# Cross-attention of layer 0 in a four-layer kernel: scores formed a second time with keys on partitions, so that the exponentials need no transpose

## The chip, the cores and the metric

The kernel is one program on one core of a Trainium2 chip. The metric is device microseconds (us) of one execution, the median of several. All numbers below come from one profiled execution of the kernel before the change, or from its three timed runs.

## The reference, cut to what matters

Four layers follow each other, each an attention from B=4 sequences of S=256 tokens (D=256) to a context of T=64 tokens. The change is in layer 0, whose keys are the 64 context tokens and the 256 tokens themselves (320 keys), with 16 heads of 16:

```python
h = jnp.concatenate([x, latents], axis=1)
q = (latents @ q_w + q_b).reshape(b, k_len, NH, DH)
kv = (h @ kv_w + kv_b).reshape(b, p + k_len, NH, DH, 2)
kmat, v = (kv[..., 0], kv[..., 1])
attn = jnp.einsum('bkhd,bnhd->bhkn', q, kmat) / DH
full_mask = jnp.concatenate([attention_mask.astype(bool), jnp.ones((b, k_len), bool)], axis=-1)
attn = jnp.where(full_mask[:, None, None, :], attn, -jnp.inf)
attn = jax.nn.softmax(attn.astype(jnp.float32), axis=-1).astype(q.dtype)
attn_out = jnp.einsum('bhkn,bnhd->bkhd', attn, v).reshape(b, k_len, H)
attn_out = attn_out @ out_w + out_b + residual
out = rmsnorm(attn_out, postnorm_w)
out = jax.nn.gelu(out @ mlp_w1 + mlp_b1) @ mlp_w2 + mlp_b2
return out + residual
```

Layers 1, 2 (two attentions) and 3 have the same pattern with other head counts and are left as they are.

## The kernel before, in words

Each engine has its own instruction stream, written out by hand, and engines meet through semaphores. A `Ring` hands out PSUM slots: three wide ones (two banks each) and two narrow ones (one bank). `take` waits until the slot's last user has drained it, so a narrow slot used by a short side product holds up the next one.

**Layer 0 attention.** A unit is one batch b, one pair of heads r (of 8) and one half q of the queries: 64 units. For each unit PE forms the scores with queries on partitions (`scores0`, L600: two matmuls of 320 columns, in wide slots 0 and 1). The two heads of a pair are kept apart by operands with zeros: `qhot` and `kpair`, which PE makes from q and k with placement matrices (`place`, L577 and L587) and ACT and DVE copy out. DVE adds the mask on 64 keys (L1316), takes the maximum (L1320) and scales it (L1321). ACT exponentiates out of PSUM with the maximum as bias and sums on the way (L1002). DVE inverts the sum (L1325), POOL multiplies (`normalize0`, L1553, into `probs`), PE transposes the result in five 128x128 pieces (`turn_probs`, L496, wide slot 2), ACT copies that out (`probs_turned`, L921), and after four units PE multiplies with the values (`values0`, L622: 20 matmuls of 128 columns with 32 columns of weights, four at a time side by side). PE runs `scores0` four units ahead.

Between the units stand side products on narrow slot 1 (`side0`): q (L541), k (L550), v (L558) and the placements for the next batch, the output projection (`proj`, L529) of the batch before. After a projection DVE adds the residual and takes statistics (`stat`, L1167 to L1172), POOL raises to the power -1/2 (`rstd_of`, L1517), DVE scales (`norm`, L1178).

**MLP of layer 0** (`mlp`, up L447, down L466): each half of the tokens is four `up` blocks of 12 matmuls of 512 columns and 96 `down` matmuls of 256. ACT applies gelu (L957), DVE splits the result in a high and a low part (L1226, L1227) and the input too (`x_parts`, L1212, L1214). Just ahead of it PE forms layer 1's keys (`keys_small`, L511), and POOL spreads them over `region` (`spread_keys`, L1559) before layer 1's scores.

SP issues nearly all loads, in order and ahead of time; during layer 0's main loop it issues nothing.

## Time and profile before

| | |
|---|---|
| three timed runs | 814.41, 817.4, 818.49 us; median 817.4 |
| the profiled execution: span | 824.4 us, 0.9% over that median |
| PE, DVE, ACT, POOL busy in it | 725.0, 535.8, 403.7, 363.0 us |
| layer 0 up to its last value product | 0 to 204.6 us |
| from there to the end of layer 0's MLP | 204.6 to 268.5 us |
| layers 1 to 3 | 268.5 to 824.4 us |

The profiled span is the first to the last instruction. Busy time counts overlapping instructions of an engine once; matmuls are pipelined, so PE can be shown busy while it only waits for the tail of a matmul.

### The profile page before, as it was taken

The page shows a single profiled execution, that of the slowest core. Times are in us where ns is not written, and L with a number is a line of the kernel's source. Part 1 is how long each engine was busy: PE and PEld are TensorE (multiplying, and loading weights), DVE is VectorE, ACT ScalarE, POOL GpSimd, SP SyncE. Part 2 cuts the span into 40 slices and gives each one's busy share as a digit, 9 for nine tenths or more (in the row PEclk, how much of TensorE's full clock was granted, in tenths as well). Part 3 has the DMA queues.
Part 4 walks back from the last instruction along what each step waited for, and adds up shares of the span by engine and source line. Part 5 has one row for each costly group of instructions (what it writes and reads, how often), then busy time and mean ns, then how long its engine had stood idle before and what let it go on. Part 6 is the DMA issues. An engine that isn't in the chain of part 4 may idle for free.

```text
span 824.4 us, 12837 instructions
## 1 busy us (share of the span) xinstructions
PE 725.0 (88%) x4752; PEld 550.8 (67%) x4752; DVE 535.8 (65%) x1034; ACT 403.7 (49%) x965; POOL 363.0 (44%) x383
## 2 busy tenths in 40 slices
PE   7888897977879878779999998999998999775798
PEld 6776676755669444548775777786576888343588
DVE  6678677664854599954546675342889567398553
ACT  3587796766411378735552222664223231476321
POOL 2386645555700488844314662000667512287200
PEclk9999998989989999979999999999999999998899
DMA  9300000000000600001533000333000000200000
GB/s 319 101 2 2 2 2 1 2 1 2 0 1 1 204 1 2 1 1 59 186 115 103 1 1 0 103 103 103 1 0 1 1 1 1 102 1 1 1 26 26
DMA packets 24957, 32.51 MB, mean 39 GB/s; under 512 B 2752, under 2 KB 19392, under 8 KB 24768
## 3 DMA queue, kind: packets, MB, share of 16 engines
q1 hardware_dynamic: 24336, 31.10, 11.2%
q10 hardware_dynamic: 560, 0.59, 0.3%
q8 instruction: 39, 0.64, 0.3%
q14 instruction: 22, 0.18, 0.1%
HBM read 30.64 MB, written 1.05 MB: 38 GB/s over the span
## 4 chain that ended last, share of the span: by engine, by line
PE 60%; DVE 19%; ACT 8%; POOL 6%; issue 6%; DMA 1%; SPq 0%; DVEq 0%; POOLq 0%; ACTq 0%
PE narrow_ps L466 8%; PE wide_ps L763 7%; PE wide_ps L447 6%; PE wide_ps L714 6%; PE narrow_ps L798 5%; PE wide_ps L496 4%; PE wide_ps L737 4%; PE wide_ps L750 4%; ACT scoresb L1002 3%; POOL probs L1539 2%; PE narrow_ps L622 2%; DVE scoresb L1241 2%; DVE mx L1250 2%; DVE sums L1257 2%; PE wide_ps L427 2%
## 5 line engine op out<-in xcount | busy, mean ns | idle before, releaser
L1531 POOL TENSOR_TENSOR scoresb<-scoresb,mx 128x768 f32<-128x768 f32 (+1 forms) x40 | 70.7, 1767 | 151.3 <-DVE mx L1248 115.3
L496 PE MATMUL wide_ps<-ident,probs 128*128 128x128 f32 x640 | 93.4, 285 | 41.4 <-POOL probs L1539 25.8
L496 PEld LDWEIGHTS wide_ps<-ident,probs 128*128 128x128 f32 x640 | 74.4, 146 | 70.3 <-issue 60.5
L1553 POOL TENSOR_TENSOR probs<-scoresb,rcp 128x512 f32<-128x512 f32 (+1 forms) x128 | 92.7, 746 | 63.9 <-DVE rcp L1325 35.0
L921 ACT ACTIVATE probsT<-wide_ps 128x1024 f32<-128x1024 f32 (+1 forms) x73 | 64.5, 883 | 111.7 <-PE wide_ps L496 111.5
L1517 POOL TENSOR_TENSOR rstd<-veps,mhalf 128x1 f32<-128x1 f32 x56 | 32.0, 571 | 133.0 <-DVE veps L1172 133.0
L1539 POOL TENSOR_TENSOR probs<-scoresb,rcp 128x1024 f32<-128x1024 f32 x40 | 78.1, 1954 | 6.4 <-DVE rcp L1258 6.4
L447 PE MATMUL wide_ps<-xq_r,wstream_r 128*128 128x512 f32 x192 | 65.4, 424 | 10.4 <-DVE xq_r L1212 6.0
L466 PEld LDWEIGHTS narrow_ps<-wstream_r,hidden 128*128 128x128 f32 x576 | 69.2, 188 | 1.2 <-DVE xB L1200 0.5
L466 PE MATMUL narrow_ps<-wstream_r,hidden 128*128 128x256 f32 x576 | 69.7, 281 | 0.3 <-DVE xB L1200 0.3
L1002 ACT ACTIVATE scoresb<-wide_ps,mx 128x320 f32<-128x320 f32 x128 | 66.8, 536 | 5.2 <-DVE mx L1321 4.9
L957 ACT ACTIVATE scoresb<-wide_ps,col 128x512 f32<-128x512 f32 x48 | 30.4, 685 | 72.6 <-PE wide_ps L447 69.9
L714 PE MATMUL wide_ps<-scoresb_r,probs_r 128*128 128x256 f32 x256 | 56.9, 305 | 4.7 <-DVE vwb L1406 4.2
L798 PE MATMUL narrow_ps<-region,probsT 128*128 128x256 f32 x256 | 58.0, 380 | 1.4 <-DVE xB L1200 1.4
L763 PE MATMUL wide_ps<-region,actT 128*128 128x512 f32 x128 | 59.0, 602 | 0.0
L1320 DVE TENSOR_REDUCE mx<-wide_ps 128x2 f32<-128x640 f32 x64 | 52.8, 824 | 2.3 <-DVE wide_ps L1316 0.2
L1359 DVE TENSOR_TENSOR wstream_r<-wstream,probs_r 128x256 fp32r<-128x256 f32 x64 | 26.7, 462 | 40.7 <-ACT probs_r L1088 40.7
L798 PEld LDWEIGHTS narrow_ps<-region,probsT 128*128 128x128 f32 x256 | 47.7, 191 | 7.5 <-DVE xB L1200 1.6
L447 PEld LDWEIGHTS wide_ps<-xq_r,wstream_r 128*128 128x128 f32 x192 | 38.4, 203 | 20.2 <-issue 11.2
L714 PEld LDWEIGHTS wide_ps<-scoresb_r,probs_r 128*128 128x128 f32 x256 | 43.1, 196 | 12.1 <-issue 6.5
L1200 DVE TENSOR_TENSOR xB<-narrow_ps,xB 128x256 f32<-128x256 f32 x48 | 20.2, 420 | 44.5 <-PE narrow_ps L466 22.9
L600 PE MATMUL wide_ps<-kpair,qhot 128*128 128x320 f32 x128 | 36.2, 366 | 9.1 <-ACT scoresb L1002 8.9
(166 smaller groups left out, 1629.6 us busy)
## 6 DMA issues: line engine op xcount, KB each, us to landing
wstream<-in_L_xattn_wk SPq DMA_DIRECT2D x8, 512.0 KB, 4.1
wstream<-in_L_xattn_wv SPq DMA_DIRECT2D x8, 512.0 KB, 5.2
wstream<-in_L_xattn_wo SPq DMA_DIRECT2D x8, 512.0 KB, 6.2
wstream<-in_wqT SPq DMA_DIRECT2D x8, 512.0 KB, 7.1
wstream<-in_L_xattn_mlp_w SPq DMA_DIRECT2D x2, 1024.0 KB, 10.6
wstream<-in_L_xattn_w_fc SPq DMA_DIRECT2D x2, 1024.0 KB, 6.2
rows<-in_rows SPq DMA_DIRECT2D x1, 1280.0 KB, 14.1
xq<-in_x SPq DMA_DIRECT2D x1, 1024.0 KB, 12.2
```

The costliest lines, as they stand in the source:

```text
L447: m = mm(ps[:, j * 512:(j + 1) * 512], w1[pw][:, kc, f * P:(f + 1) * P], xparts[px][:, kc, half * 512:(half + 1) * 512], start=kc == 0 and ...
L466: m = mm(ps[:, 0:D], hidden[:, ph, f, qoff((q + i) % 4)], w2[pw][:, f, :], start=f == 0 and part == 0, stop=f == NF - 1 and part == 2)
L496: m = nc.tensor.transpose(ps[:, j * P:(j + 1) * P], probs[:, u % 2, j * P:(j + 1) * P], ident[:])
L714: last = mm(ps[:, m * 256:(m + 1) * 256], w[:, m, kc, :], cparts[:, part, kc, :], start=kc == 0 and i == 0, stop=kc == NC - 1 and i == 2)
L763: m = mm(ps[:, g * 512:(g + 1) * 512], actT[:, c, qoff(q)], G[:, c, 8 * g:8 * g + 8, b * T:(b + 1) * T], start=c == 0, stop=c == NC - 1)
L798: mm(ps[:, 0:D], probsT[:, u % 2, r * P:(r + 1) * P], VW[:, q // 2, r, :], start=r == 0, stop=False)
L921: nc.scalar.activation(dst, src, ACT.Identity, **kw).then_inc(ring.drained[ring.slot(key)], 1)
L1002: nc.scalar.activation(scores_of(u)[:, i * KEYS0:(i + 1) * KEYS0], wide_ps[:, wide.slot(key), i * 512:i * 512 + KEYS0], ACT.Exp, scale=1.0 ...
L1320: link(v.tensor_reduce(pair_of(mx, u, 4), ps[:, :, 0:KEYS0], AX, ALU.max))
L1531: g.tensor_tensor(s3[:, first:], s3[:, first:], mx[:, u % 3, first:].unsqueeze(2).broadcast_to([P, 16 - first, n_scores]), ALU.subtract).t ...
L1539: g.tensor_tensor(probs[:, u % 2, :].rearrange("p (h k) -> p h k", h=16), s3[:, :, 0:T], rcp[:, u % 3, :].unsqueeze(2).broadcast_to([P, 16 ...
L1553: g.tensor_tensor(probs[:, u % 2, o:o + 2 * n].rearrange("p (i k) -> p i k", i=2), s3[:, :, lo:hi], pair_of(rcp, u).unsqueeze(2).broadcast ...
```

## The change: what it does

The scores are now formed twice. A group is one batch b and four pairs of heads (c): eight groups of four steps, 32 steps in all, a step being one pair with all 256 queries.

1. **Operands through DRAM.** q and k of a group are written to two scratch tensors in DRAM (`store_qk`, six DMAs) and read back with a head's 16 dimensions, in three copies of high and low parts, on 48 partitions, heads of a pair at partitions 0 and 64 (`load_qk`, six DMAs). A row of `krow` holds the mask, a row of ones in `krow` meets a row of `qrow` that holds minus the maximum. The placement matrices, `qhot` and `kpair` are gone.
2. **Scores for the maximum** (`max_scores0`): three matmuls (64, 320 and 256 columns) for each half of the queries, always in wide slot 2. DVE takes the maximum (`max0`). Every two steps PE transposes these maxima (side product "max"), ACT negates them into `maxrow`, and SP copies them with two DMAs into `qrow` (`load_max`), two steps before they are used.
3. **Scores with keys on partitions** (`scores0`): four matmuls of 256 columns, and two more in every other step for the context keys, in quarters of wide slots 0 and 1. ACT exponentiates whole banks (512 elements), without sums.
4. **Value products** read these exponentials. The sum over keys is a product with ones: `values0` has eight rounds (k = 0 to 7) of four matmuls of 256 columns, spread over the steps 1 to 3 of the next group. Rounds 5 and 6 read `keysum`, the sum of two key blocks that POOL forms (`sum_keys0`). For all but the first group POOL waits before these until the value products of the group before are finished.
5. **Division at the end** (`attended0`): DVE inverts the sums (128x256, out of PSUM) and multiplies. Unit order, the transposes, the normalisation on POOL and the copies of the turned probabilities are gone from layer 0.
6. **Around it**: loads for later are issued between the groups (`late_loads`); layer 1's small weights are loaded after the last value product; `keys_small` for layer 1, and with it `spread_keys`, stands in the middle of layer 0's MLP; the MLP's first input half is split after the last norm and no longer in the loop.

```diff
-        units0 = [(b, 4 * c + j, q) for b in range(B) for c in range(NC) for q in range(2) for j in range(4)]
+            jobs = []
+            if p in (0, 2) and 0 < 2 * g + p // 2 + 1 < 2 * GROUPS0:
+                jobs.append(("max", 2 * g + p // 2 + 1))
+            if g + 3 < GROUPS0 and p in (0, 1):
+                jobs.append(("qk"[p], g + 3))
+            if g % 2 and p == 2 and g + 1 < GROUPS0:
+                jobs.append(("v", (g + 1) // 2))
+            if g % 2 and 3 <= g < GROUPS0 and p in (1, 3):
+                jobs.append(("proj", g - 3 + p // 2))
...
+        VALUES0 = {1: (0, 3), 2: (3, 6), 3: (6, 8)}
...
+            for step in range(STEPS0 + 5):
+                g, p = divmod(step, PAIRS0)
+                if step < STEPS0:
+                    scores0(step)
+                units = max_units(step)
+                if units:
+                    max_scores0(*units[0])
+                jobs = side0(step)
+                for job in jobs[:1]:
+                    side_product0(job, SIDE)
+                if 0 < g <= GROUPS0 and p in VALUES0:
+                    values0(g - 1, VALUES0[p])
+                if units:
+                    max_scores0(*units[1])
+                for job in jobs[1:]:
+                    side_product0(job, SIDE)
...
+            def load_max(half):
+
+                g, r = half // 2, half % 2 * 2
+                sp.wait_ge(*narrow.empty(("max", half)))
+                for i in range(2):
+                    sp.dma_start(qrow[64 * i + MAX_ROW:64 * i + MAX_ROW + 1, g % 3, r:r + 2, :].bitcast(F32),
+                                 maxrow[2 * i:2 * i + 2, half % 2, :].bitcast(F32)).then_inc(max_loaded[half % 2], 16)
...
+            for g in range(GROUPS0):
+                load_max(2 * g + 1)
+                if g + 2 < GROUPS0:
+                    load_qk(g + 2)
+                if g + 1 < GROUPS0:
+                    load_max(2 * g + 2)
+                if g + 3 < GROUPS0:
+                    store_qk(g + 3)
+                late_loads(g)
...
+                link(v.reciprocal(denominv[:], ps[:, S:2 * S]))
+                v.tensor_tensor(qT[:, c, b * S:(b + 1) * S], ps[:, 0:S], denominv[:], ALU.mult
+                                ).then_inc(narrow.drained[narrow.slot(key)], 1)
...
+            for step in range(STEPS0 + 5):
+                g, p = divmod(step, PAIRS0)
+                units = max_units(step)
+                if units:
+                    max0(*units[0])
+                jobs = side0(step)
+                for job in jobs[:1]:
+                    side0_copy(job)
+                if 0 < g <= GROUPS0 and p == 3:
+                    attended0(g - 1)
+                if units:
+                    max0(*units[1])
+                for job in jobs[1:]:
+                    side0_copy(job)
...
+            def sum_keys0(step):
+
+                g = step // PAIRS0
+                for i in range(2):
+                    pool.wait_ge(*quarter.empty(("S", step, i)))
+                if g:
+                    pool.wait_ge(*narrow.full(("ao", 0, *group0(g - 1))))
...
+                if step < STEPS0:
+                    sum_keys0(step)
+                for job, n in side0(step):
+                    if job == "proj":
+                        rstd_of(0, n)
```

On PE, in the main loop of before, one unit reads as follows: transposes of one unit, scores of another, side products, and every four units the value products.

```order
L496 MATMUL wide_ps<-ident,probs 128x128 x5
L600 MATMUL wide_ps<-kpair,qhot 128x320 x2
L577 MATMUL narrow_ps<-qparts,place 128x256 x4
L496 MATMUL wide_ps<-ident,probs 128x128 x5
L600 MATMUL wide_ps<-kpair,qhot 128x320 x2
L587 MATMUL narrow_ps<-kparts,place 128x320 x2
L587 MATMUL narrow_ps<-kparts,place 128x192 x2
```

After the change, PE in the last step of group 3 (an odd group): scores (L595, L603), first maximum unit (L576), projection (L523), the last two value rounds (L638), second maximum unit.

```order
L595 MATMUL wide_ps<-qrow,krow 128x256 x4
L603 MATMUL wide_ps<-qrow,krow 128x256 x2
L576 MATMUL wide_ps<-krow,qrow 128x64
L576 MATMUL wide_ps<-krow,qrow 128x320
L576 MATMUL wide_ps<-krow,qrow 128x256
L523 MATMUL narrow_ps<-wstream,xq 128x256 x2
L638 MATMUL narrow_ps<-keysum,ones 32x256 x4
L638 MATMUL narrow_ps<-wsmall,ones 32x256 x4
L576 MATMUL wide_ps<-krow,qrow 128x64
L576 MATMUL wide_ps<-krow,qrow 128x320
L576 MATMUL wide_ps<-krow,qrow 128x256
```

The transposes have left and two score products per step have come; the second maximum unit stands behind the projection and the value rounds.

On DVE one unit of before is four short instructions:

```order
L1316 TENSOR_TENSOR wide_ps<-wide_ps,mask 128x2x64
L1320 TENSOR_REDUCE mx<-wide_ps 128x2
L1321 TENSOR_SCALAR mx<-mx 128x2
L1325 RECIPROCAL rcp<-sums 128x2
```

After the change, DVE from the end of the third step of group 3 to the end of the group: maximum, then norm, residual and statistics of a projection, then the division, then the next maxima.

```order
L1407 TENSOR_REDUCE mx<-wide_ps 128x2
L1270 TENSOR_SCALAR xn<-xB,rstd 128x256
L1292 TENSOR_TENSOR xB<-narrow_ps,xB 128x256
L1259 BN_STATS stats<-xB 128x6
L1260 BN_AGGR mv<-stats 128x2
L1262 SCALAR_TENSOR_TENSOR mv<-mv 128x1
L1264 TENSOR_SCALAR veps<-mv 128x1
L1416 RECIPROCAL denominv<-narrow_ps 128x256
L1417 TENSOR_TENSOR xq<-narrow_ps,denominv 128x256
L1407 TENSOR_REDUCE mx<-wide_ps 128x2 x3
```

The norm (L1270), and the division of 256 columns, now stand between two maxima.

On POOL, after the change, the four steps of group 3: the key sums (L1649) with row additions (L1606) between them, and each projection's power (L1610) behind the sum of its step.

```order
L1649 TENSOR_TENSOR keysum<-probsT 128x512
L1606 TENSOR_TENSOR xq<-xq,rows 128x256
L1649 TENSOR_TENSOR keysum<-probsT 128x512
L1610 TENSOR_TENSOR rstd<-veps,mhalf 128x1
L1606 TENSOR_TENSOR xq<-xq,rows 128x256
L1649 TENSOR_TENSOR keysum<-scoresb 128x512
L1606 TENSOR_TENSOR xq<-xq,rows 128x256
L1649 TENSOR_TENSOR keysum<-scoresb 128x512
L1610 TENSOR_TENSOR rstd<-veps,mhalf 128x1
```

Before, POOL's power stood between normalisations; now the first of these powers is queued behind two sums that wait for the value products of the group before.

## Rows read from the trace of the kernel before

**Rows 1.** Windows: length, busy us of PE, PEld, DVE, ACT, POOL, clock, DMA

```profile
0.00:41.80 41.80, 34.05 (x159) 27.82 (x163) 25.92 (x57) 19.92 (x51) 14.07 (x29) 0.92 0.62 207
41.80:204.60 162.80, 134.55 (x1285) 106.82 (x1284) 114.87 (x295) 124.21 (x339) 97.73 (x139) 0.93 0.01 2
204.60:232.30 27.70, 18.10 (x84) 13.86 (x74) 23.82 (x20) 10.70 (x16) 15.20 (x4) 0.88 0.00 0
232.30:268.50 36.20, 36.19 (x242) 33.07 (x243) 15.34 (x20) 5.07 (x8) 0.00 (x0) 0.95 0.00 1
```

**Rows 2.** Timeline of one unit: start us, us, engine and instruction [idle before]

```profile
102.51 0.23 ACT L1002 ACTIVATION_READ_ACCUMULATOR scoresb<-wide_ps,mx 128x1 f32 x1
...
102.79 0.56 PE L600 MATMUL wide_ps<-kpair,qhot 128*128 128x320 f32 x2 [0.25 <-ACT scoresb L1002]
...
103.44 0.28 DVE L1316 TENSOR_TENSOR wide_ps<-wide_ps,mask 128x128 f32<-128x128 f32 x1
```

**Rows 3.** Groups by line and form, first 270 us: busy, mean ns | idle before

```profile
L1553 POOL TENSOR_TENSOR probs<-scoresb,rcp 128x512 f32<-128x512 f32 x64 | 66.9, 1046 | 63.9 <-DVE rcp L1325 35.0 <-PE wide_ps L496 28.9
L1320 DVE TENSOR_REDUCE mx<-wide_ps 128x2 f32<-128x640 f32 x64 | 52.8, 824 | 2.3 <-DVE wide_ps L1316 0.2
L921 ACT ACTIVATE kpair<-narrow_ps 128x512 fp32r<-128x512 f32 x16 | 9.6, 601 | 7.9 <-PE narrow_ps L587 7.7
L1200 DVE TENSOR_TENSOR xB<-narrow_ps,xB 128x256 f32<-128x256 f32 x8 | 3.3, 418 | 7.9 <-PE narrow_ps L529 7.8
L1268 DVE MEMSET qhot<- 128x4096 f32 x1 | 3.5, 3472 | 0.8 <-issue 0.8
```

**Rows 4.** Chain that ended last: start us, us, piece (fp32 matmuls count double)

```profile
39.20 1.73 PE narrow_ps L541 x8
...
41.76 1.23 PE narrow_ps L622 x40
42.99 1.47 PE narrow_ps L550 x8
...
237.26 11.39 PE narrow_ps L466 x96
248.65 8.43 PE wide_ps L447 x36
```

**Rows 5.** Two lines of reciprocals: duration ns min/median/max

```profile
L1325 DVE RECIPROCAL rcp<-sums x64: 150/158/168, 18.7 to 198.7; 128x2 f32<-128x2 f32 x64
...
L1258 DVE RECIPROCAL rcp<-sums x40: 253/253/255, 289.6 to 757.1; 128x16 f32<-128x16 f32 x40
```

**Rows 6.** DMA issues, first 80 us: KB each, median us to landing

```profile
probs<-in_mask_BxS_ik ACTq DMA_DIRECT2D x1, 128.0 KB, 7.0
...
actT<-in_xT SPq DMA_DIRECT2D x1, 256.0 KB, 4.6
col<-in_cols ACTq DMA_DIRECT2D x1, 192.0 KB, 3.1
```

**Rows 7.** Timeline of the start and of the end of layer 0's attention

```profile
6.08 3.75 PE L541 MATMUL narrow_ps<-actT,wstream 128*128 128x256 f32 x8 [0.81 <-DMA actT<-in_xT]
...
205.56 1.10 PE L529 MATMUL narrow_ps<-wstream,xq 128*128 128x256 f32 x4 [0.69 <-ACT xq L921]
208.32 0.55 POOL L1517 TENSOR_TENSOR rstd<-veps,mhalf 128x1 f32<-128x1 f32 x1 [7.12 <-DVE veps L1172]
208.90 0.35 DVE L1178 TENSOR_SCALAR xn<-xB,rstd 128x256 f32<-128x256 f32 x1 [0.66 <-POOL rstd L1517]
...
211.47 14.14 POOL L1559 TENSOR_TENSOR region<-headbuf,head 128x4096 f32<-128x4096 f32 x2
211.54 7.15 DVE L1178 TENSOR_SCALAR xn<-xB,rstd 128x256 f32<-128x256 f32 x1 [0.66 <-POOL rstd L1517]
...
218.61 7.55 DVE L1226 CAST hidden<-scoresb 128x1024 fp32r<-128x1024 f32 x1
226.20 1.23 DVE L1227 TENSOR_TENSOR hidden<-scoresb,hidden 128x1024 fp32r<-128x1024 f32 x1
```

More of the change, by code:

```diff
@@ L366, in done1, with max_units @@
+        START0 = [("q", 0), ("k", 0), ("q", 1), ("k", 1), ("v", 0), ("q", 2), ("k", 2), ("vctx", 0), ("vctx", 1)]
+        def max_units(step):
+            half = step // 2 + 2
+            return [(half, step % 2, qh) for qh in range(2)] if half < 2 * GROUPS0 else []
+        START_MAX0 = [(half, pl, qh) for half in range(2) for pl in range(2) for qh in range(2)]
+        VALUES0 = {1: (0, 3), 2: (3, 6), 3: (6, 8)}
         def done1(step):
@@ new lines, in take_quarter, with scores0 @@
+            def take_quarter(key):
+                s, before = quarter.take(key, 1, (0, 1, 2, 3))
+                if before:
+                    pe.wait_ge(quarter.drained[s], before)
+                return quarter_ps[:, s, :], quarter.filled[s]
+            def scores0(step):
+                g, r = divmod(step, PAIRS0)
+                half = step // 2
+                tiles = [take_quarter(("S", step, i)) for i in range(2)]
+                pe.wait_ge(max_loaded[half % 2], 32 * (half // 2 + 1))
+                for kb in range(2):
+                    for i in range(2):
+                        k0 = 64 * i
+                        m = mm(tiles[i][0][:, kb * S:(kb + 1) * S],
+                               krow[k0:k0 + MAX_ROW + 1, g % 3, r, (kb + 1) * P:(kb + 2) * P],
+                               qrow[k0:k0 + MAX_ROW + 1, g % 3, r, :], start=True, stop=True)
+                        if kb == 1:
+                            m.then_inc(tiles[i][1], 1)
+                if r % 2:
+                    ps, filled = take_quarter(("C", step // 2))
+                    for i in range(2):
+                        m = mm(ps[:, i * S:(i + 1) * S], krow[:, g % 3, r - 1 + i, 0:P], qrow[:, g % 3, r - 1 + i, :], start=True, stop=True)
+                    m.then_inc(filled, 1)
@@ L874, in _ @@
+            sp.wait_ge(*narrow.full(("ao", 0, B - 1, NC - 1)))
             sp.dma_start(*halves(q_w1, t["L1_xattn_Wq"])).then_inc(load["w1"], 16)
@@ L963, in mlp @@
                             norm_turned(*turned, (1,))
+                        if i == NF // 2 and between:
+                            between()
             def probs_turned(u):
@@ new lines, in side0_copy @@
+                if kind == "proj":
+                    stream_norm(0, n, n - 1 if n else None, ("proj", 0, n), xB, 0)
+                    return
+                dve.wait_ge(*narrow.full(job))
+                ps = narrow_ps[:, narrow.slot(job), :]
+                done = narrow.drained[narrow.slot(job)]
+                if kind in ("q", "k"):
+                    parts, size = (qparts, S) if kind == "q" else (kparts, KEYS0)
+                    _, drained = narrow.empty(job)
+                    dve.wait_ge(done, drained - 1)
+                    v.scalar_tensor_tensor(out=parts[:, n % 2, 1, :], in0=ps[:, 0:size],
+                                           scalar=column(f"L0_{kind}_b", n % NC),
+                                           in1=parts[:, n % 2, 0, :].bitcast(F32), op0=ALU.add, op1=ALU.subtract
+                                           ).then_inc(done, 1)
@@ L1350, in _ @@
+            norm(0, NQ - 1)
+            x_parts(0, 0, [narrow.empty(("ln", c)) for c in range(NC)])
             mlp(0, 0, lambda q: add_residual(("down", 0, q), xA, q, 1))
```

612 lines of the change are left out of this document (301 added, 311 removed).

## The prediction

> **What bounds the kernel now.** I read the windows by stage first. Layer 0's main loop, from its first value product to its last, runs from 41.8 to 204.6 us; in these 162.8 us PE is busy 134.6, ACT 124.2, DVE 114.9, POOL 97.7, at a clock of 0.93, with almost no DMA [rows 1]. No engine is full: each unit goes PE, DVE, ACT, POOL, PE, ACT, and what is lost is lost in these handovers. The stage before takes 41.8 us with DMA share 0.62, and from the last value product to the end of the MLP there are 63.9 us, of which the last 36.2 are all PE [rows 1]. The other layers, 555.9 us, don't change, so the forecast is: when does layer 0's MLP end, instead of at 268.5.
>
> **Prices.** A handover from PE: two matmuls issued at 102.79 reach DVE at 103.44; less their streaming (640 columns, 0.30 at the 0.119 us per 256 columns of L466, 11.39 us over 96) it is 0.35. Back, ACT ends at 102.74 and PE starts at 102.79: 0.05 [rows 2, 4]. The maximum over 640 elements keeps its 0.82 [rows 3]. q for one c is half of 1.73, so 0.87; k is 1.47; v has q's full 1.73; a projection 1.10 [rows 4, 7]. A value round of four matmuls of 128 columns takes 1.23/5 = 0.25, so one of 256 columns about 0.44 [rows 4]. ACT takes 0.60 for 512 elements [rows 3]. POOL's sum of 512 elements: 1.05, the row addition between not more than 0.75 by POOL's size-to-time, the power 0.55 [rows 3, 7]. Residual plus statistics: from 206.66 (end of L529) to POOL at 208.32, 1.65; a norm 0.35 [rows 7].
>
> **What is removed.** 80 transposes, 48 placement matmuls and their copies per batch, a POOL multiply of over 1 us per unit [rows 3], two ACT copies. PE's work of the new loop by the prices: scores 32 steps of five matmuls, 19 us; maxima 56 units of 640 columns, 17 to 20; value rounds 64 at 0.44, 28; maxima transposed, q, k, v, projections, 31. Together about 97. ACT per step: 2.5 passes of 0.60 and some copies, 2 us. So neither PE nor ACT fills the loop. Why I don't expect the loop at PE's rate follows.
>
> **The serial chain through one slot.** All maximum units use wide slot 2. PE streams a unit (0.35), DVE gets it 0.35 later, reduces 0.84, and PE may write again 0.05 later: 1.6 us a unit, two per step, 3.2 us per step at least for 28 steps, if DVE is free. It is not always free, and PE has its own order. I lay out one even group with q and k (PE times from its first maximum unit). Step 0: unit 0 to 0.35, maxima transposed to 0.8, unit at 1.6 to 1.95, q to 2.8. Step 1: scores to 3.5, unit to 3.8, k (waits for q's two copies) 4.2 to 5.7, three value rounds to 7.0, unit to 7.3. DVE reduces that to 8.5. Step 2: scores, unit at 8.6, transposes and three rounds to 10.7, unit to 11.05, reduced at 12.24. Step 3: unit at 12.3, two rounds to 13.5, unit to 14.25; but DVE first divides.
>
> **The division.** No row has an inverse of 256 elements. Two elements take 0.158, sixteen 0.253 [rows 5], 6.8 ns an element, so 256 take 1.9 us; the other bound is the 0.42 of an ordinary 256-element operation out of PSUM [rows 3]. I take 1.9, since the slope is the same instruction's. With the multiply, DVE is away 13.9 to 16.3, and the group's last maximum ends at 17.2. One even group costs 17.2 us. The VectorE page of the Trainium skill (VectorE: DVE Perf Modes, "why 8 slices") says that the inverse is an iterative divide with a repeat count of 8; the slope in the row agrees.
>
> **A wait of POOL that DVE inherits.** In odd groups from 3 on, a projection stands in step 1 and another in step 3. Before the second, DVE must norm the first, which needs POOL's power; POOL has it behind the key sums of steps 0 and 1 of this group, and these wait until the previous group's value rounds end, in step 3. So DVE stands in step 3 from about 15.8; rounds end 16.95; POOL sum, row addition, sum, power: 20.3; norm, residual, statistics 22.5; division 24.9; last maximum 25.8. Behind DVE wait PE's next maximum unit and everything after it. Group 3 costs 25.8 us, group 5 (no q and k, no row addition) 23. Without this wait they would be about 20 and 18.
>
> **Sum of the loop.** Group 0 (no values, no division) 12.8; group 1 19 (v); 2: 17.2; 3: 25.8; 4: 17.2; 5: 23; 6, without q and k: 12.3 to its last PE work; group 7, without maxima, about 10, then POOL two sums and the power, DVE projection and division, and eight rounds of 0.44, together 21 until the last value product. The sum is 148.3 us from the first scores of the loop to the last value product.
>
> **The start.** x lands at 6 us and q is formed at half clock (3.75 us for eight matmul records against 1.73 later) [rows 4, 7]. DVE zeroes 7,680 elements at 3.47 us per 4,096 [rows 3], 6.5 us, so its first low part is at about 11. q and k of two groups are then passed through two narrow slots, to 15; six stores and six loads follow at about 0.5 us issue each, and land 3.1 to 4.6 us later, as the least loaded rows do [rows 6]: near 23. Eight maximum units of 1.75 (low clock) to 37, transposing, negating and the DMA of the row: first scores at 42. The last value product comes at 42 + 148.3 = 190.3 instead of 204.6, 14.3 us earlier.
>
> **The MLP.** From the last value product: division 2.9, projection and residual, then the last projection, statistics, power, norm, splitting the input: first `up` 10.8 us later. `up` of half 0 and first of half 1 with transposes 14.9 (12 matmuls at 8.43/36 each), `down` 11.4, keys 1.9, `up` 8.4, `down` 11.4: 48.0 [rows 4]. And `spread_keys` (14.14 us on POOL) now falls in the second half. In the trace a norm and a cast of DVE that met it took 7.15 and 7.55 us, the norm instead of 0.35 [rows 7]. In the new place it meets the hidden split of blocks 1 and 2, on which `down` waits: if only the casts are held, PE loses 4.6 us; if the subtraction (L1227) is too, 7.5. In the trace L1227 began when POOL was through [rows 7], so it tells neither; I take 7.5, as L1227 reads the same tiles. The page SBUF — State Buffer of the Trainium skill (section on the shared port pair) says that a DVE operation with two SBUF inputs is held by a GpSimd one that reads SBUF, which would give 7.5. Sum 10.8 + 48.0 + 7.5 = 66.3 against 63.9: 2.4 lost.
>
> **Together.** 14.3 - 2.4 = 11.9 us less: 812.5 of 824.4, or 1.44%. On the median of 817.4 that is 805.6. I say 806.
>
> **Rivals.**
> *Waits shorter than laid out.* If the inverse takes 0.42 instead of 1.9, seven divisions return about 10 us. If DVE's wait for POOL is hidden, another 10. Matmuls on partitions 0 and 64 may also run side by side, as the four-column-strip ones of L622 do in the trace (four in 0.25 us) [rows 4]; 9 us of PE, partly hidden. Between 15 and 30 us less than 812.5 gives 776 to 790 on the median. The page TensorE: Matmul & The Clock Gate of the Trainium skill (Part 3, packing) says that tiles in different row groups run concurrently. No row here has such a pair.
> *PE sets the pace.* A loop of 103 us in place of 148.3: 812.5 - 45, or 761 on the median. Against it speaks the single slot, 3.2 us per step.
> *The maximum row comes late (slower).* A row goes PE, ACT, SP, DMA, and back to PE, where all scores wait for it, and ACT behind. Its transposes end near 0.8 in step 0, ACT has to finish the step's exponentials (to 2.4), two issues 0.9; scores of step 2 stand at 7.3 to 8. So a landing of up to about 4 us is free; with the 3.1 of the least loaded row there is 1 us to spare, with the 7.0 of a row in the busy start [rows 6] 15 halves lose up to 3 each, 45 us, less what DVE's waits cover, say 30: 842, or 835 on the median. Against it: the traffic per group is 1.7 MB, not the 8.7 MB of the first 41.8 us (207 GB/s) [rows 1]. For it: these DMAs follow 1 MB loads in one queue. The page DMA: Bandwidth & Descriptors of the Trainium skill (Anatomy of one DMA) gives about 2 us as a fixed cost, by which the row would be in time and the forecast holds.
> *The clock falls.* PE waits more than before. If its clock falls to 1.2 GHz for half of the loop's matmuls where the loop is PE's, some 12 us are lost and the time is 814 to 820.
>
> **How the numbers follow.** The forecast's own range is 798 to 812, chance 0.36. Shorter waits, 0.23; PE's pace 0.04; clock 0.14; late maxima, or more of the kind of wait that I found on POOL, 0.23. Faster by over 0.5% (about what a measurement of this kernel can tell from none): 0.63; same 0.14; slower 0.23. The range 776 to 838 leaves out PE's pace, the lowest of the shorter waits and the worst of the late maxima.
>
> **What the profile would show.** Right: the last value product near 190; DVE's maxima with idle time before them; DVE waiting on rstd in steps 15 and 23, some 4 us each; an inverse of about 1.9 us; the first scores near 42; a cast of 7 us in the MLP's second half. Wrong: scores waiting on a DMA (late maxima), an inverse below 1 us, PE matmuls of `scores0` at under 0.1 us spacing, or layers 1 to 3 longer than 555.9 us.

## The result and the profile after

The changed kernel takes 863.6 us (median of 4 runs, 860.8 to 867.7) against 817.9 of the kernel before (4 runs, 814.4 to 820.9): a ratio of 1.054 (95% interval 1.049 to 1.060). It is slower; the forecast was 806 us, range 776 to 838. (A ratio leaves out executions over 1.5% above the fastest of the same kernel, as two of the four of the run pool_edge are, its profiled one among them.) The profiled execution has a span of 863.3 us (before 824.4) and a mean granted clock of PE of 0.893 (before 0.957), where 1.00 is 2.4 GHz and 0.50 is 1.2 GHz.

The windows by stage of the changed kernel, to be read against [rows 1]: start and end, length, then busy us (and count) of PE, PEld, DVE, ACT, POOL, the granted clock, DMA share, GB/s.

```profile
0.00:47.80 47.80, 27.68 (x104) 20.98 (x104) 22.95 (x30) 4.86 (x9) 4.96 (x20) 0.70 0.55 159
47.80:233.30 185.50, 144.70 (x1016) 89.30 (x1016) 83.38 (x123) 56.06 (x109) 54.05 (x54) 0.72 0.28 81
233.30:304.70 71.40, 55.97 (x314) 48.01 (x315) 40.38 (x44) 15.07 (x23) 16.37 (x6) 0.88 0.04 10
304.70:863.30 558.60, 503.98 (x3000) 368.48 (x2998) 355.95 (x643) 243.03 (x552) 235.22 (x212) 0.97 0.13 42
```

ACT, DVE and POOL did lose work in the loop (56, 83 and 54 us busy; before 124, 115 and 98). PE is *busier*, 144.7 us against 134.6, with a fifth fewer matmuls, and its clock is 0.72 where it was 0.93. By stage: first scores 5.8 us later than forecast (47.8, not 42), the loop 37.2 longer (185.5, not 148.3), the way to the end of the MLP 5.1 longer (71.4, not 66.3), the other layers 2.7 longer. Those four make the 50.8 us between 863.3 and the sum of 812.5.

The same matmuls at both levels of the clock (timeline of the changed kernel: start, us; the windows of these rows give a clock of 0.50, 1.00, 0.50 and 1.00). q takes 2.07 us at 1.2 GHz and 1.03 at 2.4; four matmuls of the scores 0.80 and 0.51.

```profile
13.60 2.07 PE L540 MATMUL narrow_ps<-actT,wstream 128*128 128x256 f32 x4 [0.69 <-DVE qparts L1380]
...
20.41 1.03 PE L540 MATMUL narrow_ps<-actT,wstream 128*128 128x256 f32 x4
...
47.81 0.80 PE L595 MATMUL wide_ps<-qrow,krow 50*128 50x256 f32 x4 [2.78 <-DMA qrow<-maxrow]
...
123.70 0.51 PE L595 MATMUL wide_ps<-qrow,krow 50*128 50x256 f32 x4
```

Who waited for whom in the loop (view of waits, 47.8 to 233.3: us in total, times, longest). PE waits for DVE's maxima, DVE for PE's units, and DVE three times for POOL's power. The maximum row comes further down the list: PE's wait for its DMA is 2.8 us in the whole loop, all of it at the first scores. (PEld's 3.3 us for the same DMA, in the same view, is the same wait.)

```profile
DVE mx L1407 <- PE wide_ps L576: 51.4, 46, 4.1
...
PE wide_ps L576 <- DVE mx L1407: 31.0, 18, 9.0
DVE xn L1270 <- POOL rstd L1610: 18.2, 3, 8.6
```

The longest of these waits, at the end of group 3 (timeline). POOL's key sum has waited 16.5 us for the value rounds, the power comes behind two sums, the norm behind the power, then residual, statistics and the inverse of 1.75 us; the maximum at 140.75 frees the slot for which PE has waited 9.00 us.

```profile
132.16 1.26 POOL L1649 TENSOR_TENSOR keysum<-probsT 128x512 f32<-128x512 f32 x1 [16.49 <-PE narrow_ps L638]
...
135.28 0.55 POOL L1610 TENSOR_TENSOR rstd<-veps,mhalf 128x1 f32<-128x1 f32 x1
135.80 0.72 POOL L1606 TENSOR_TENSOR xq<-xq,rows 128x256 f32<-128x256 f32 x1
135.87 0.81 DVE L1270 TENSOR_SCALAR xn<-xB,rstd 128x256 f32<-128x256 f32 x1 [5.11 <-POOL rstd L1610]
...
138.63 1.75 DVE L1416 RECIPROCAL denominv<-narrow_ps 128x256 f32<-128x256 f32 x1
...
140.75 0.81 DVE L1407 TENSOR_REDUCE mx<-wide_ps 128x2 f32<-128x640 f32 x1
141.62 0.79 PE L576 MATMUL wide_ps<-krow,qrow 49*128 49x64 f32 x3 [9.00 <-DVE mx L1407]
```

### The profile page after: what moved, and what is told of

The parts are those of the page before. It is cut to its first block, busy times and chain, and to the rows that moved or that the text cites. A ratio compares the mean times of both kernels' runs of the same rounds, so it can differ in the third digit from the quotient of the medians.

```text
span 863.3 us, 11707 instructions
## 1 busy us (share of the span) xinstructions
PE 732.3 (85%) x4432; PEld 526.8 (61%) x4432; DVE 502.7 (58%) x840; ACT 319.0 (37%) x693; POOL 310.6 (36%) x292
## 4 chain that ended last, share of the span: by engine, by line
PE 60%; DVE 22%; POOL 5%; issue 4%; DMA 4%; ACT 3%; SPq 2%; ACTq 0%; POOLq 0%; DVEq 0%
PE narrow_ps L459 8%; PE wide_ps L790 7%; PE wide_ps L440 6%; PE narrow_ps L825 5%; PE narrow_ps L638 5%; PE wide_ps L576 4%; PE wide_ps L741 4%; DMA wstream<-in_wqT 3%; PE wide_ps L777 3%; PE wide_ps L490 3%; DVE mx L1407 3%; PE wide_ps L764 2%; DVE scoresb L1334 2%; DVE mx L1343 2%; POOL probs L1633 2%
## 5 line engine op out<-in xcount | busy, mean ns | idle before, releaser
L1012 ACT ACTIVATE probsT<-wide_ps 128x1024 f32<-128x1024 f32 x40 | 40.9, 1023 | 105.3 <-PE wide_ps L490 105.3
L459 PE MATMUL narrow_ps<-wstream_r,hidden 128*128 128x256 f32 x576 | 71.9, 285 | 8.0 <-DVE hidden L1319 7.7
L576 PE MATMUL wide_ps<-krow,qrow 49*128 49x64 f32 (+2 forms) x192 | 41.7, 451 | 42.5 <-DVE mx L1407 37.5
L1610 POOL TENSOR_TENSOR rstd<-veps,mhalf 128x1 f32<-128x1 f32 x56 | 32.0, 572 | 121.1 <-DVE veps L1264 121.1
L490 PEld LDWEIGHTS wide_ps<-ident,probs 128*128 128x128 f32 x320 | 39.5, 151 | 48.2 <-issue 47.5
L490 PE MATMUL wide_ps<-ident,probs 128*128 128x128 f32 x320 | 46.3, 292 | 26.5 <-POOL probs L1633 24.7
L576 PEld LDWEIGHTS wide_ps<-krow,qrow 49*128 49x128 f32 x192 | 26.0, 248 | 63.7 <-DVE mx L1407 49.8
L741 PE MATMUL wide_ps<-scoresb_r,probs_r 128*128 128x256 f32 x256 | 54.4, 295 | 7.6 <-DVE vwb L1499 4.2
L825 PEld LDWEIGHTS narrow_ps<-region,probsT 128*128 128x128 f32 x256 | 47.8, 191 | 7.5 <-DVE xB L1292 1.6
L741 PEld LDWEIGHTS wide_ps<-scoresb_r,probs_r 128*128 128x128 f32 x256 | 41.5, 188 | 16.3 <-issue 10.9
L1649 POOL TENSOR_TENSOR keysum<-scoresb 128x512 f32<-128x512 f32 x15 | 19.1, 1279 | 85.0 <-ACT scoresb L1096 51.1
L440 PEld LDWEIGHTS wide_ps<-xq_r,wstream_r 128*128 128x128 f32 x192 | 37.2, 198 | 20.0 <-issue 11.6
```

Of the source, the lines that this page charges most:

```text
L440: m = mm(ps[:, j * 512:(j + 1) * 512], w1[pw][:, kc, f * P:(f + 1) * P], xparts[px][:, kc, half * 512:(half + 1) * 512], start=kc == 0 and ...
L459: m = mm(ps[:, 0:D], hidden[:, ph, f, qoff((q + i) % 4)], w2[pw][:, f, :], start=f == 0 and part == 0, stop=f == NF - 1 and part == 2)
L490: m = nc.tensor.transpose(ps[:, j * P:(j + 1) * P], probs[:, u % 2, j * P:(j + 1) * P], ident[:])
L576: m = mm(ps[:, i * 512 + to:i * 512 + to + hi - lo], qrow[k0:k0 + MAX_ROW, g % 3, r, qoff(qh)], krow[k0:k0 + MAX_ROW, g % 3, r, lo:hi], st ...
L741: last = mm(ps[:, m * 256:(m + 1) * 256], w[:, m, kc, :], cparts[:, part, kc, :], start=kc == 0 and i == 0, stop=kc == NC - 1 and i == 2)
L825: mm(ps[:, 0:D], probsT[:, u % 2, r * P:(r + 1) * P], VW[:, q // 2, r, :], start=r == 0, stop=False)
```

## The experiments

Theories after the result. **Clock**: PE's own work, right in amount, runs at half clock for over half of the loop (the expectations call this the main theory). **Chain**: the one slot of the maximum units and DVE's waits set the time whatever the clock is. **Row**: the maximum row's DMA is late. **POOL**: DVE's wait for the power. Ratios are to the kernel before, timed along with each run (its medians 819 to 822 us); the changed kernel's own is 1.054. Differences between runs are given by medians; an interval of a ratio is some 0.5 to 0.9% to either side, so a difference below about 1% (8 us) between two runs is not clear of noise. Every run has one profile, of one of its executions. In the edits, `...` marks what is cut.

**Work for PE where it waits (warm2).** Four places like this one, ahead of PE's waits:

```
                 tiles = [take_quarter(("S", step, i)) for i in range(2)]
+                fill(tiles[0][0], 2)
```

Here `fill` is two transposes of the identity into a PSUM tile that PE holds.

> Adds 126 transposes of the identity (two at a time, 0.42 us each at half clock, 0.21 at full) into PSUM that PE alone holds, ahead of the scores, the maxima's transposes, the first value round and the eight maximum units of the start, so that PE works where it waited for DVE. If the loss is the clock (main theory), the granted clock of the loop rises from 0.72 to above 0.85, the four-strip value rounds fall from 634 ns a matmul towards 379, and the kernel takes 835 to 855 us in spite of the added work. If the serial chain of maximum units and DVE's waits set the time by themselves (rival), nothing comes back, and the added 20 to 40 us of PE make it 865 to 895. If the maximum row's DMA is late (rival), it stays within 1% of the changed kernel.

875.4 us, ratio 1.064 (1.057 to 1.072): slower than the changed kernel, as the chain theory said, and the clock of the loop is 0.73, not above 0.85. In the profile PE was busy without a gap from 66 to 78 us and the clock stayed at 0.50 (windows of warm2):

```profile
66.00:72.00 6.00, 6.00 (x25) 3.83 (x26) 1.92 (x3) 1.93 (x4) 0.00 (x0) 0.50 0.73 235
72.00:78.00 6.00, 6.00 (x27) 4.21 (x31) 1.83 (x3) 2.10 (x4) 0.00 (x0) 0.50 0.79 193
```

So the first form of the clock theory, that PE's waiting keeps the clock down and any work lifts it, fell here. What remained open was whether the low clock itself costs the time.

**Without the row (norow).**

```
-                pe.wait_ge(max_loaded[half % 2], 32 * (half // 2 + 1))
...
-                for i in range(2):
-                    sp.dma_start(qrow[64 * i + MAX_ROW:64 * i + MAX_ROW + 1, g % 3, r:r + 2, :].bitcast(F32),
...
```

> Leaves out the subtraction of the maximum: maxima are formed and transposed as before, but the row is not moved by the four DMAs of a group, and no score waits for it. If the late row is what costs (rival), the kernel falls by 15 us or more, below 850. By the trace of the changed kernel the scores wait for it 6.1 us in two places, so the main theory and the serial-chain rival both expect 856 to 864.

860.3 us, ratio 1.049 (1.042 to 1.055). (The 6.1 us in the expectation count one wait twice, on PE and on PEld.) First scores come at 45.2, not 47.8, and the groups keep their lengths within 0.4 us but for group 6, 2.7 shorter, and group 7, 1.3 longer. By the medians the row costs under 1%. This theory is out as the main cause.

**Without the maximum (nomax).** All maximum units, their transposes and the rows are left out.

> Leaves out the maximum altogether: no maximum units, transposes, row copies or row DMAs; exponentials are of unshifted scores. It gives what forming the scores a second time costs in this arrangement. If that second forming (its chain PE to DVE and what it does to the clock) is the cause, the loop shrinks from 185.5 us to 110 to 130 and its clock is above 0.85: 780 to 810 us in all. If the loss lies in POOL's and DVE's other waits and in the storing and loading of q and k, the loop stays above 150 us: 825 or more.

795.9 us, ratio 0.972 (0.964 to 0.981). The time is in the range of the expectation; the loop is not quite (133.6 us, 31.6 to 165.2, for 110 to 130), nor is its clock (0.78 for above 0.85). Forming the scores twice costs about 8% (0.972 against 1.054), some 67 us, of which 16.2 us are a later start (first scores at 31.6). Even with the maximum for nothing this arrangement saves only 3%. It could have been more: here a wait grows that is 7.3 us in the changed kernel, POOL's residual rows behind a DMA and PE behind POOL (waits of nomax, 58 to 84 us).

```profile
POOL xB L1597 <- DMA rows<-in_rows: 18.3, 1, 18.3
...
PE narrow_ps L635 <- POOL keysum L1640: 15.5, 1, 15.5
```

**POOL's power earlier (pool).** Ahead of the key sums of step 0 (and no longer behind those of step 1):

```
...
+                if p0 == 0 and g0 % 2 and 3 <= g0 < GROUPS0:
+                    rstd_of(0, g0 - 3)
                 if step < STEPS0:
                     sum_keys0(step)
                 for job, n in side0(step):
-                    if job == "proj":
+                    if job == "proj" and not (p0 == 1 and step < STEPS0):
```

> Moves POOL's power for the projection of step 1 of groups 3, 5 and 7 ahead of that group's key sums, so that DVE's norm of step 3 does not wait until the previous group's value rounds end. The prediction's ledger puts the wait at 5 to 6 us in groups 3 and 5: 852 to 858 us if the wait is all that goes; 840 to 850 if it also lifts the clock (main theory); within 0.5% of the changed kernel if PE's pace at the low clock covers the wait.

850.6 us, ratio 1.035 (1.028 to 1.042): 13 us by the medians or 1.8% by the ratios less than the changed kernel; in the profile the last value product comes at 221.4, not 233.3. PE's wait for maxima falls from 31.0 to 21.8 us. The wait was the one forecast, and its price was right in sum: 3.8 us come back in groups 3 and 4, 5.5 in 5 and 6 and 4.0 in 7 (the ledger has 5.8 + 5 in the first two pairs), less 1.6 that groups 1 and 2 are longer. The clock of the loop stays at 0.72, and 850.6 lies between the two ranges expected. With the wait gone, what stands at each group's end is the division: the second maximum of step 3 waits behind 1.76 + 0.42 us, and PE for it (timeline of pool).

```profile
87.13 0.49 PE L576 MATMUL wide_ps<-krow,qrow 49*128 49x64 f32 x3
87.27 1.76 DVE L1416 RECIPROCAL denominv<-narrow_ps 128x256 f32<-128x256 f32 x1 [0.20 <-PE narrow_ps L638]
...
89.06 0.42 DVE L1417 TENSOR_TENSOR xq<-narrow_ps,denominv 128x256 f32<-128x256 f32 x1
89.41 0.81 DVE L1407 TENSOR_REDUCE mx<-wide_ps 128x2 f32<-128x640 f32 x1
90.28 0.79 PE L576 MATMUL wide_ps<-krow,qrow 49*128 49x64 f32 x3 [2.42 <-DVE mx L1407]
```

All further runs but short and keys, which start from the changed kernel, start from pool.

**The maximum ahead of the division (pool_div).**

```
-                if 0 < g <= GROUPS0 and p == 3:
-                    attended0(g - 1)
                 if units:
                     max0(*units[1])
+                if 0 < g <= GROUPS0 and p == 3:
+                    attended0(g - 1)
```

> The kernel of the run pool, with DVE reducing the second maximum unit of step 3 of each group before it divides the values, not after. The trace of pool has PE waiting 2.4 to 3.9 us at each group's first unit for that reduction, which stands behind 1.76 + 0.42 us of division. By the serial-chain theory the division then only delays the next unit's reduction, and 0.5 to 1 us a group return: 843 to 847 us. If the shorter idle stretch also keeps the clock up (main theory, second form): 825 to 840 us.

842.1 us, ratio 1.028 (1.022 to 1.035), 8.5 us less than pool; the intervals of the two ratios overlap. In the profile the last value product is at 210.1, 11 us earlier, and the loop's first seven groups have a clock of 0.77 for 0.70. The time lies between the range of the chain theory (843 to 847) and that of the clock theory (825 to 840).

**No division at all (pool_nodiv).** A copy stands in for the reciprocal.

> The kernel of the run pool with a copy in place of the reciprocal (values are not divided by the sums): 0.42 us in place of 1.75, seven times in the loop and once behind it. By the chain alone it returns 8 x 1.33 = 10.6 us: 840 us. If PE's shorter wait at each group's first unit (2.4 to 1.1 us) also keeps the clock up: 825 to 835 us.

834.4 us, ratio 1.016 (1.012 to 1.021): 1.9% or 16 us below pool, where the chain alone gives 10.6, and 18.8 us in the profile (last value product at 202.5). Groups 5 and 6 run at 1.00 and 0.89 and take 17.2 and 15.8 us, against 20.5 and 20.4 at 0.83 and 0.67. In these profiles a shorter wait returned more than itself.

**A cheaper maximum (short).** DVE reduces 2 x 64 columns.

```
-  ps[:, :, 0:KEYS0], AX, ALU.max
+  ps[:, :, 0:64], AX, ALU.max
```

> The changed kernel with DVE reducing 2 x 64 columns of each maximum unit, not 2 x 320 (a maximum over a fifth of the scores): by the slope of other reductions about 0.25 us in place of 0.82, with PE's work as it was. The serial-chain theory (3.2 us a step) says that 64 x 0.57 = 36 us of it go: 825 to 832 us. If PE's work at the low clock sets most steps (main theory), only the waits of PE for that reduction shrink (31 us of them in the loop, and 8 x 0.57 = 4.6 in the start), by some 15 to 20 in all: 843 to 850 us, with the granted clock of the loop still below 0.8.

846.2 us, ratio 1.033 (1.026 to 1.040): 17 us below the changed kernel of the 36 that the chain theory gave (some 4 of them in the start, first scores at 43.7). DVE's busy time between the first scores of group 0 and of group 7 fell from 73.4 to 44.3 us, the stretch from 158.9 to 146.2, its clock is 0.73.

**Both (light).** The edits of short and pool_nodiv on top of pool.

> The kernel of the run pool with both DVE edits of the runs short and pool_nodiv (a maximum over a fifth of the columns; values not divided). PE's work is as it was. If DVE's chain is what sets the time, the loop falls towards PE's own 97 to 105 us: 775 to 790 us. If PE's work at the low clock sets it, the two savings add to less than the sum of the single ones (17 + 16 us below the changed kernel's 864 and pool's 851): 815 to 825 us, with the loop's clock below 0.9.

822.1 us, ratio 1.001 (0.997 to 1.004). The windows from the first scores of group 0 to those of group 7 of the changed kernel, of pool and of light:

```profile
47.81:206.67 158.86, 127.68 (x848) 80.05 (x850) 73.39 (x107) 49.10 (x96) 43.02 (x44) 0.70 0.33 95
```

```profile
47.62:198.75 151.13, 129.31 (x849) 80.92 (x851) 73.55 (x107) 49.11 (x96) 42.98 (x44) 0.70 0.35 100
```

```profile
44.47:175.83 131.36, 120.89 (x849) 76.02 (x850) 39.70 (x107) 49.01 (x96) 44.00 (x44) 0.74 0.41 115
```

With DVE at 39.7 us PE is busy 120.9 of 131.4 us: now it is mostly PE that sets the loop, at a clock of 0.74. Of PE's busy time 81.1, 84.5 and 66.7 us lie in stretches at 0.50 (summed stretch by stretch from the three profiles); with these halved its work in full-clock microseconds is the same in all three: 87.1, 87.1 and 87.6. The chain theory, which had the loop fall to 97 to 105 us here (it is 148.2 to the last value product), is out as the whole cause; the clock theory's size held (815 to 825).

**The clock lifted with DVE's chain as it is (pool_start, pool_start24, pool_edge, warm_all).** Matmuls of 128 rows and 256 columns into a bank that PE alone holds. In pool_start and pool_start24 there are two after each of the start's eight units, then 10 or 24 ahead of the first scores. In pool_edge there are 8 ahead of the first unit of groups 1 to 6. warm_all is pool_start24 with 10 there and four more in step 2 of groups 0 to 6.

```
+            def fill(ps, g, n):
+                for _ in range(n):
+                    mm(ps[:, 0:S], krow[:, g % 3, 0, 0:P], qrow[:, g % 3, 0 if g else 3, :], start=True, stop=True)
```

> The kernel of the run pool, with two extra matmuls of 128 rows and 256 columns after each of the start's eight maximum units and ten after the maxima are transposed, all in a bank that PE alone holds, where PE waits for DVE and for the maximum row. In the changed kernel the clock is 0.50 from 30 to 76 us. If the idleness of the start sets that (main theory, second form), the clock is full when the first scores run, and groups 0 and 1 end about 10 us earlier: 838 to 845 us. Rival: no change or up to 5 us more than the 850.6 of pool.

> pool_start with 24 extra matmuls ahead of the first scores in place of ten: about 5 us later in the start at half clock, or less if the clock rises in them. If the clock is what makes group 0 take 17.6 us, it takes 13.1 again with its clock at 1.00 in the profile, and the whole is 844 to 849 us. If 13.1 was chance: 17.6 again, and 852 to 856.

> The kernel of the run pool, with eight extra matmuls (128 rows, 256 columns, about 0.21 us each at full clock) into a bank that PE alone holds, ahead of the first maximum unit of groups 1 to 6: there PE waits 2.4 to 3.9 us for DVE, which divides. It leaves DVE's chain as it is and adds 48 matmuls, 10 us at full clock. If those idle stretches are what drops the clock (main theory, second form), the clock no longer falls at the group boundaries, the loop's mean rises from 0.74 to above 0.85 and the time falls to 830 to 842 us. If only DVE's chain counts (rival), or if something other than idleness holds the clock down, it stays within 0.5% of the 850.6 us of pool or rises by up to 10.

> pool_start24 with ten extra matmuls ahead of the first maximum unit of groups 1 to 6 and four ahead of that of step 2 of groups 0 to 6 (88 in all, 18 us at full clock). DVE's chain is unchanged. Main theory: the clock is above 0.85 over the loop, and groups 1 to 3 take 18 to 21 us in place of 22 to 24.5 in spite of the extra matmuls: 835 to 848 us. Rival (DVE's chain and PE's own work set the time, the clock costs nothing): groups as in pool, 5 to 18 us more than pool: 855 to 868.

pool_start 845.2 us, ratio 1.032 (1.025 to 1.038); pool_start24 845.5, 1.030 (1.023 to 1.037); pool_edge 831.9 to 845.5, 1.022 (1.010 to 1.033); warm_all 840.5, 1.022 (1.016 to 1.029). All have more PE work than pool and none is slower than its 1.035, but all four intervals overlap with pool's, that of warm_all only just. The expectations hold in part: the loop's clock is 0.76 in pool_edge and 0.83 in warm_all, not above 0.85, and groups 1 to 3 of warm_all take 23.2, 21.3 and 20.9 us, not 18 to 21. The groups of the profiles say more. Group 0, the same instructions in both, in pool and in pool_start24 (windows):

```profile
47.62:65.20 17.58, 15.81 (x64) 10.84 (x66) 6.71 (x9) 7.07 (x14) 5.07 (x4) 0.50 0.24 60
```

```profile
49.71:62.32 12.61, 9.33 (x66) 6.58 (x66) 6.71 (x9) 6.89 (x14) 5.06 (x4) 0.95 0.30 78
```

PE 15.8 us busy at 0.50, 9.3 at 0.95, and the group 17.6 or 12.6 us; the ledger has 12.8. DVE's work is 6.71 us in both. Group 3, in pool and in warm_all, where it carries 14 extra matmuls and still takes 3.7 us less:

```profile
109.39:133.91 24.52, 21.72 (x147) 13.84 (x147) 12.95 (x24) 6.94 (x14) 8.22 (x9) 0.79 0.45 135
```

```profile
107.97:128.84 20.87, 19.37 (x162) 13.08 (x161) 13.04 (x24) 7.07 (x14) 8.27 (x9) 1.00 0.54 160
```

That the low clock itself costs time is shown by these two pairs, and by a third below.

**The two together, and more (div_start, div_start_edge, best).** Edits of pool_div and pool_start; the same with six extra matmuls at the start of groups 1 to 6; and pool_start24 with the division moved on to step 0 of the second group after.

> The two edits of the runs pool_div and pool_start together on top of pool. They returned 8.5 and 5.4 us by their medians; if they are independent, 836 to 838 us.

> The kernel of the run div_start with six extra matmuls ahead of the first maximum unit of groups 1 to 6, as in pool_edge. If covering idle stretches keeps the clock (pool_edge held it at 1.00 from 151 to 181 us, in one group of six), another 3 to 8 us go: 829 to 835 us; it still doesn't reach the kernel before (about 820), since groups 0 and 1 run at half clock with PE busy all the time. Rival: the extra matmuls, now no longer covered by a wait of 2.4 us, cost what they bring: 836 to 842 us.

> The kernel of the run pool_start24 with DVE dividing a group's values in step 0 of the second group after it, behind the first maximum, while PE forms q. pool_div returned 8.5 us; this gives another 2 to 4 if the division is covered by q: 832 to 840 us. It doesn't come below the kernel before (about 819), since groups 1 to 7 still take half their time at half clock.

div_start 842.3 us, ratio 1.027 (1.020 to 1.033): not better than pool_div, and not the 836 to 838 expected. Its profile tells a reason: the same extra matmuls that lifted the clock in the profile of pool_start didn't here. Group 0 of pool_start, then of div_start:

```profile
48.46:61.54 13.08, 10.04 (x65) 7.08 (x66) 6.71 (x9) 6.89 (x14) 5.09 (x4) 0.87 0.30 81
```

```profile
47.93:65.50 17.57, 15.80 (x64) 10.83 (x66) 6.71 (x9) 7.07 (x14) 5.07 (x4) 0.50 0.23 59
```

The two programs are the same instruction for instruction until the end of group 0: their edits differ first in group 1, where DVE divides for the first time. DVE's work is 6.71 us in both, PE's 10.0 us at 0.87 and 15.8 at 0.50, and the group 13.1 or 17.6 us. With the same instructions in the same order, the 4.5 us between them are the cleanest measure of the clock here.

div_start_edge 838.4, 1.022 (1.017 to 1.028), as the rival said. best 835.7, 1.018 (1.012 to 1.023), with the last value product at 206.7, two microseconds behind the kernel before; the MLP then loses the rest (72.4 us from there to its end, before 63.9). By its ratio it is the fastest version that computes everything, though the intervals of div_start_edge and warm_all overlap with its own, and it is still slower than before.

**The keys back ahead of the MLP (keys).**

```
-            mlp(0, 0, small_keys1)
+            small_keys1()
+            mlp(0, 0)
```

> The changed kernel with layer 1's keys formed and spread ahead of layer 0's MLP again, as in the kernel before, not between its halves. Layer 0's attention does not change. The ledger of the MLP (48.0 us of PE, 10.8 ahead of it, 7.5 for the subtraction that waits for POOL) says that 5 to 8 us return: 856 to 859 us. Rival: POOL's work then meets the first half's splits instead, and nothing returns: 862 to 866 us.

867.8 us, ratio 1.058 (1.051 to 1.065): nothing returned, as the rival said. From the last value product to the end of the MLP there are 72.0 us (232.4 to 304.4), with the change 71.4. POOL's 14.5 us meet the first half's splits here and the second half's there, and PE waits 8.3 or 7.5 us.

## Why the prediction was wrong

*Prices* and *Sum of the loop*: the step that failed. Every PE price was taken from rows at a granted clock of 1.00 (windows of the kernel before), and the loop was summed with them. The amount of work was nearly right: of the changed loop's 144.7 us of busy PE 88.3 lie in stretches at 0.50 and 56.4 in stretches at 1.00, and 88.3 / 2 + 56.4 = 100.6 us at full clock, against about 97 in the prediction. (This takes busy time to double at half clock, as q's does; that the same sum gives 87 to 88 us in three profiles under light bears it out.) The low clock turned it into 144.7 us, 44.1 more, and the ledger's amount was 3.6 short: together 47.7. PE's waits were shorter than the ledger's, 40.8 us against 148.3 - 97 = 51.3, since slower matmuls fill part of them: + 47.7 - 10.5 = 37.2 us, the whole excess of the loop. So "neither PE nor ACT fills the loop" holds at full clock only. By groups, first scores to first scores (group 7: to the last value product):

| group | ledger | changed | pool | light | warm_all (extra matmuls in it) |
|---|---|---|---|---|---|
| 0 | 12.8 | 17.6 | 17.6 | 16.4 | 13.0 |
| 1 | 19 | 21.2 | 22.2 | 21.1 | 23.2 |
| 2 | 17.2 | 21.4 | 22.0 | 18.9 | 21.3 |
| 3 and 4 | 43.0 | 52.3 | 48.5 | 41.5 | 42.6 |
| 5 and 6 | 35.3 | 46.4 | 40.9 | 33.4 | 39.1 |
| 7 | 21 | 26.6 | 22.6 | 16.8 | 22.7 |

*The clock falls*: the right mechanism, as a rival with 0.14 and "some 12 us"; it was given half of the loop's matmuls "where the loop is PE's". It needed the question the other way round: a loop that isn't PE's at full clock becomes PE's, in good part, at half. Group 0 alone lost 4.5 to 5 us. How much a full clock throughout would return isn't shown, since no run reached one (warm_all came to 0.83). An estimate from two of the pairs above: 5.0 us came back for 0.45 more clock over 17.6 us, 3.7 for 0.21 more over 24.5 us; the loop lacks 0.28 over 185.5 us, which scales to 33 to 37 us. That would be nearly the whole excess, but it is argued, not run.

*The serial chain through one slot*: its prices held (the reduction 0.82 us, and PE starts the next unit some 0.05 us after it ends), but it bound the loop only in part: cutting each reduction from 0.82 to 0.29 us (run short) returned 17 us. *The division*: 1.75 us each (forecast 1.9), and where it stood it was behind PE's waits of 2.1 to 2.4 us at the first unit of groups 2, 3 and 5. *A wait of POOL that DVE inherits*: right in place and kind. In groups 3 and 5 it was 5.1 and 4.5 us, where the prediction has some 4; a third, of 8.6 us, stands in group 7. PE meets the first two at the next group's first unit (9.0 and 8.3 us).

*The start*: first scores at 47.8, not 42. The first unit waits 4.9 us for krow until 31.35, 8.4 us later than the 23 forecast, of which 2.5 came back behind it. The first k had to wait for ctxT until 10.1, and the loads of krow stand on SP behind the second group's stores, six stores and six loads of a group taking 3.9 to 4.7 and 4.4 to 4.6 us to issue (0.6 to 0.8 each, not 0.5). Units at 1.71 us were as forecast (1.75). The "half clock" at which the prediction has the first q is read from its 3.75 us alone; the window of that row (6.08 to 9.83) gives 1.00.

*The MLP*: PE's wait for the held subtraction was 7.5 us, as forecast. The Trainium skill (page SBUF — State Buffer, section on the shared port pair) says that a DVE instruction with two SBUF inputs contends with a GpSimd one that reads SBUF, and this trace agrees: a cast of 4.46 us (0.68 just before POOL began) and then the subtraction of two SBUF inputs, 7.96 instead of 1.23, beside POOL's two instructions of 14.53 in all (timeline of the changed kernel).

```profile
275.81 14.53 POOL L1654 TENSOR_TENSOR region<-headbuf,head 128x4096 f32<-128x4096 f32 x2 [33.58 <-ACT headbuf L1012]
...
278.97 4.46 DVE L1318 CAST hidden<-scoresb 128x1024 fp32r<-128x1024 f32 x1 [3.52 <-ACT scoresb L1051]
...
283.47 7.96 DVE L1319 TENSOR_TENSOR hidden<-scoresb,hidden 128x1024 fp32r<-128x1024 f32 x1
...
291.48 0.80 PE L459 MATMUL narrow_ps<-wstream_r,hidden 128*128 128x256 f32 x2 [7.51 <-DVE hidden L1319]
```

But it isn't a loss of the new place: the run keys shows one as long in the old place. The 5.1 us beyond the forecast are mostly the clock again, in two places. `up` of the first half and the first block of the second took 18.5 us (243.07 to 261.59), not 14.9: the clock was 0.50 until 248.0, and the first eleven matmuls took 5.0 us at prices that give 2.6. Behind the wait of 7.5 us it was 0.50 again, until 295.8, and the rest of `down` took 13.2 us, where its 90 matmuls have 10.7 (windows of the changed kernel).

```profile
243.07:248.08 5.01, 5.01 (x12) 3.61 (x12) 0.97 (x1) 0.00 (x0) 0.00 (x0) 0.50 0.00 0
248.08:261.59 13.51, 12.81 (x59) 9.87 (x57) 10.28 (x11) 9.17 (x13) 0.00 (x0) 1.00 0.01 1
291.48:304.70 13.22, 13.01 (x92) 12.70 (x93) 4.87 (x7) 0.00 (x0) 0.00 (x0) 0.84 0.01 1
```

The rest of the first is waits of PE for DVE's splits; the way to the first `up` was 1.0 us shorter than forecast.

*The maximum row comes late*: it didn't, but for the first, for which PE waited 2.8 us. SP issued its two DMAs from 45.47 us on and PE began at 47.81, 2.3 us later, less than the 3.1 of the least loaded row in [rows 6]; all later ones were in time. *Waits shorter*, first part: matmuls of the scores on partitions 0 and 64 do run side by side. Four of 256 columns take 0.34 us to the next matmul at full clock (123.70, next at 124.04), less than the 4 x 0.119 = 0.48 of [rows 4]. It did not bring the loop's work below the 97 us of the ledger.

## What to carry to other kernels

Before summing a ledger of a loop with PE prices, ask what the sum is at half clock: if PE's work doubled would fill the loop, as the 97 us here would, the forecast needs that case as one of its likeliest, not as a tail. In this kernel the matmuls added for the maxima hand over to DVE each time, PE stood still for 40.8 of 185.5 us (before, 28.2 of 162.8), and the price showed as longer matmuls, not as waits. A wait at a group's end is worth looking for first: moving one POOL instruction returned 1.8%, and one swap on DVE another 0.6% by the ratios (11 us in the profile), the latter not clear of noise.

## What the hardware showed that I had not expected

The granted clock doesn't follow PE's busy share in the records. In group 0 PE was busy 15.8 of 17.6 us at 0.50 throughout; in pool_start24 it held 0.95 over the same group while busy 9.3 of 12.6 us. In the changed kernel's loop the clock fell seven times (at 91.0, 111.5, 135.4, 162.7, 186.6, 210.5 and 224.1 us), each time during or within 2 us of a wait of PE of 2.1 to 9.0 us, and came back in the middle of later work. Yet in warm2 it fell at 62.3 us, where PE's one wait over 0.2 us since the first scores had been 0.78 us. The same start, with the same ten extra matmuls, ended at full clock in the profile of pool_start and at half clock in that of div_start. What brings it back is open.

Executions of one kernel differ in the same way: those of the changed kernel run from 860.8 us at a mean clock of 0.901 to 867.7 at 0.887, and those of pool_edge from 831.9 at 0.930 to 845.5 at 0.915.
